# A vision block on one core: one array for each group's rows, and the issue lists of four engines written anew

## The reference, cut to what matters

```python
h = tok(x, W)                                  # patches @ W.T, class token in front
def attn(x):                                   # on layernorm(h)
    k, v, sr = ln1(x) @ Wk.T, ln1(x) @ Wv.T, sigmoid(ln1(x) @ Wr.T)
    y = bi_wkv(decay / T, first / T, k, v)     # two scans with a running maximum, both ways
    x = x + sr * y @ Wo.T
    return x + sigmoid(ln2(x) @ Wr_f.T) * (square(relu(ln2(x) @ Wk_f.T)) @ Wv_f.T)
h = h + attn(layernorm(h))
h = h + moe(layernorm(h))     # sum over experts of c[t, e] * (silu(x Wg + bg) * (x Wu + bu)) Wd, and the shared one
```

## Time and profile before

| | us |
|---|---|
| median of 3 runs | 268.33 |
| lowest, highest | 268.15, 270.0 |
| the profiled execution, its own time | 268.65 |
| its span, first to last instruction | 266.8 |

### The profile page before, as it was taken

One profiled execution on the slowest core, in us unless ns is written; L12 is line 12 of the kernel. 1 busy time (PEld: TensorE's weight loads), 2 busy tenths in 40 slices (PEclk: granted clock), 3 DMA queues, 4 the chain that ended last, 5 costly groups with the idle time before them and its releaser, 6 DMA issues.

```text
span 266.8 us, 4316 instructions
## 1 busy us (share of the span) xinstructions
PE 233.7 (88%) x1436; PEld 211.5 (79%) x1436; DVE 195.0 (73%) x496; ACT 147.6 (55%) x305; POOL 18.0 (7%) x24
## 2 busy tenths in 40 slices
PE   0484968588878999999999999999999999999994
PEld 0373428465557899998999999999999999899993
DVE  4459898999997999989986599877731445654442
ACT  2489886989449997462756894144444332122220
POOL 4100402030011000030010000101000010000000
PEclk9998699999999999999999999999999999999999
DMA  5679550000000280000002430000014510014311
GB/s 150 210 254 337 176 184 2 0 0 0 0 2 1 47 195 2 2 0 0 4 26 68 174 105 4 0 1 0 2 30 160 164 37 2 1 35 106 68 34 37
DMA packets 12823, 17.49 MB, mean 66 GB/s; under 512 B 2144, under 2 KB 10882, under 8 KB 12674
## 3 DMA queue, kind: packets, MB, share of 16 engines
q1 hardware_dynamic: 11272, 16.20, 20.7%
q10 hardware_dynamic: 1530, 1.02, 1.4%
HBM read 16.22 MB, written 0.99 MB: 65 GB/s over the span
## 4 chain that ended last, share of the span: by engine, by line
PE 65%; DVE 16%; ACT 9%; issue 5%; DMA 2%; POOL 1%; SPq 0%; DVEq 0%; POOLq 0%; ACTq 0%
PE PG L958 17%; PE PA L978 15%; PE PG L960 11%; PE PF L978 4%; PE PA L1162 3%; DVE S L721 3%; PE PQ L958 2%; PE PX L995 2%; PE PF L995 2%; DVE K L745 2%; DMA w_tok<-in_w_tok 2%; PE PF L985 1%; DVE S L726 1%; DVE hid L901 1%; POOL rstd L374 1%
## 5 line engine op out<-in xcount | busy, mean ns | idle before, releaser
L553 ACT ACTIVATE act<-PG,columns 128x222 f32<-128x222 f32 (+3 forms) x56 | 28.4, 506 | 63.7 <-PE PG L960 60.0
L958 PE MATMUL PG<-stack,hi_egu 128*128 128x222 f32 (+1 forms) x288 | 62.1, 324 | 0.8 <-DVE hid L901 0.5
L901 DVE SCALAR_TENSOR_TENSOR hid<-PG,columns,act 128x222 f32<-128x222 f32 (+1 forms) x52 | 27.1, 520 | 30.9 <-PE PG L960 15.7
L958 PEld LDWEIGHTS PG<-stack,hi_egu 128*128 128x128 f32 x288 | 45.2, 190 | 4.9 <-DVE hid L901 2.9
L978 PE MATMUL PA<-w_ed,hid 128*124 128x192 f32 (+1 forms) x240 | 46.0, 327 | 0.7 <-DVE hid L914 0.7
L960 PE MATMUL PG<-stack,lo_egu 128*128 128x222 f32 (+1 forms) x192 | 42.7, 304 | 0.0
L978 PEld LDWEIGHTS PA<-w_ed,hid 128*124 128x124 f32 (+1 forms) x240 | 38.6, 183 | 1.1 <-issue 1.0
L960 PEld LDWEIGHTS PG<-stack,lo_egu 128*128 128x128 f32 x192 | 31.7, 190 | 0.0
L374 POOL TENSOR_TENSOR rstd<-var,minus_half 112x2 f32<-112x2 f32 (+3 forms) x12 | 15.2, 1266 | 198.7 <-DVE var L647 198.7
L914 DVE TENSOR_TENSOR hid<-hid,gates 128x222 f32<-128x222 f32 (+1 forms) x48 | 21.7, 463 | 8.2 <-DMA gates<-c_rows 7.4
L978 PE MATMUL PF<-w_down,mix_hid 128*124 128x192 f32 (+1 forms) x120 | 23.2, 327 | 0.2 <-ACT mix_hid L525 0.2
(11 more groups left out here) (230 smaller groups left out, 418.6 us busy)
## 6 DMA issues: line engine op xcount, KB each, us to landing
gates<-in_w_egu SPq DMA_DIRECT2D x6, 512.0 KB, 4.0
gates<-c_rows SPq DMA_DIRECT2D x16, 138.8 KB, 2.8
gates<-c_rows SPq DMA_DIRECT2D x16, 92.5 KB, 2.7
w_ed<-in_w_ed SPq DMA_DIRECT2D x1, 1152.0 KB, 8.0
gates<-c_rows SPq DMA_DIRECT2D x12, 83.2 KB, 2.8
...
```

What stands on the lines that cost most here:

```text
L553: nc.scalar.activation(act[128 - gate:128, n % 2, 0:G.n], PG[0:gate, gate_bank(n), 0:G.n], ACT.Silu, bias=bias).then_inc(act_silu, 1)
L901: V_.scalar_tensor_tensor(out, PG[part, 1, 0:G.n], bias, act[part, i, 0:G.n], ALU.add, ALU.mult).then_inc(mul_done, 1)
L958: mm(out, w_hi[:, slot, cols], x[:, p, 0:G.n], start=(p == 0), stop=False, skip_group_check=True)
```

## The change

1. **One array per group.** `stream[g]` takes the place of `h0`, `base` and `h1`. `x1` adds into it, `h1` adds into it, the experts add into it, and it is stored from there. The two waits named above are gone.
2. **In place.** `norm2` is `x1`, `norm3` is `gate_r`. `Zm` is the front of `V`. ReLU goes from PSUM to `mix_hid` and the square works there in place, so `relu` is gone, and the wait for the mix matmul two before stands ahead of ReLU, not ahead of the square. New waits: `x0` of group g waits for the transposes (not the norm) of M of the group before, and `vt` for the `o` matmuls of the group before.
3. **Gates.** The array holds `HELD` = 4 periods of three chunks, which is all 12 chunks, so slots, DMAs and waits come out as they were. The formulas for tiles and banks also give the same numbers for 2 and 3 tiles.
4. **Queue of SP.** `patches(3)` stands ahead of `gates_across(0)`.
5. **Lists.** The three lists are written anew.

```diff
+        stream = [sb(f"h_{g}", [G.tp, G.tiles, C]) for g, G in enumerate(GROUP)]
-        norm = [None, *(sb(f"norm{i}", [TP, TILES, C]) for i in (1, 2, 3))]
+        norm = [None, sb("norm1", [TP, TILES, C]), x1, gate_r]
-        Zm = sb("Zm", [128, N])
+        Zm = V[:, 0:N]
...
             patches(2)
+            patches(3)
             gates_across(0)
-            patches(3)
...
                 act_e.wait_ge(pe_tok, at(pe_tok, g, bank + 1))
-                if g >= 2 and bank == 0:
-                    act_e.wait_ge(x1_ready, at(x1_ready, g - 2, 1))
...
             yield "kt"
+            since(act_e, pe_o, g)
             tails(V, upper, upper)
...
-            since(act_e, norm_ready[2], g)
+            since(act_e, pe_transposed[2], g)
...
-                nc.scalar.activation(relu[:, 0:G.n], PQ[:, 0:G.n], ACT.Relu).then_inc(act_relu, 1)
-                act_e.wait_ge(act_relu, at(act_relu, g, m + 1))
                 if m >= 2:
                     act_e.wait_ge(pe_mix, at(pe_mix, g, m - 1))
...
+                nc.scalar.activation(mix_hid[:, m % 2, 0:G.n], PQ[:, 0:G.n], ACT.Relu).then_inc(act_relu, 1)
+                act_e.wait_ge(act_relu, at(act_relu, g, m + 1))
+                nc.scalar.activation(mix_hid[:, m % 2, 0:G.n], mix_hid[:, m % 2, 0:G.n], ACT.Square).then_inc(act_square, 1)
...
-            if g >= 2:
-                v.wait_ge(out_stored[g - 2], 16 * GROUP[g - 2].tiles)
...
 ACT_ORDER = _order(
...
-    "F2:exps F2:weights Y0:e6 F3:tok0 Y0:e7 M1:rf M1:mix0 Y0:e8 M1:mix1 Y0:e9 M1:mix2 M1:mix3 M1:mix4 Y0:e10 F3:ln1 M1:mix5",
...
+    "Y0:e5 F3:tok0 M1:rf M1:mix0 Y0:e6 M1:mix1 Y0:e7 F2:weights M1:mix2 Y0:e8 M1:mix3 Y0:e9 M1:mix4 Y0:e10 Y0:e11 F3:ln1",
```

More of the change, by code:

```diff
@@ L41, in __init__ @@
         last = self.n - self.tp
-        self.ts = [0, last] if self.tiles == 2 else [0, last // 4 * 2, last]
-        self.banks = ((0, 0, 2), (1, 2, 3))[:self.tiles - 1]
+        self.ts = [last * t // (2 * (self.tiles - 1)) * 2 for t in range(self.tiles)]
+        self.banks = [(a // 2, a, min(a + 2, self.tiles)) for a in range(0, self.tiles, 2)]
         self.rounds = len(self.banks)
@@ L116, in build, with gate_slot @@
         whole = {name: sb(f"w_{name}", [p, n, C]) for name, p, n in WHOLE}
-        gates = sb("gates", [128, ECH, N])
-        flat_gates = gates[:, :, :].rearrange("p c n -> p (c n)")
-        raw = [flat_gates[:, i * RING_COLS:(i + 1) * RING_COLS] for i in range(RING)]
+        gates_raw = sb("gates", [128, max(3 * HELD * N, RING * RING_COLS)])
+        gates = gates_raw[:, 0:3 * HELD * N].rearrange("p (c n) -> p c n", n=N)
+        raw = [gates_raw[:, i * RING_COLS:(i + 1) * RING_COLS] for i in range(RING)]
+        def gate_slot(g, chunk):
+            return (g * ECH + chunk) % (3 * HELD)
         columns = sb("columns", [128, sum(n for _, n in COLUMNS)])
@@ L140, in build @@
         pat = sb("pat", [128, 2, N])
-        h0 = [sb(f"h0_{i}", [TP, TILES, C]) for i in range(2)]
+        stream = [sb(f"h_{g}", [G.tp, G.tiles, C]) for g, G in enumerate(GROUP)]
         x1, gate_r = (sb(n, [TP, TILES, C]) for n in ("x1", "gate_r"))
-        base, h1 = ([sb(f"{n}_{i}", [TP, TILES, C]) for i in range(2)] for n in ("base", "h1"))
-        norm = [None, *(sb(f"norm{i}", [TP, TILES, C]) for i in (1, 2, 3))]
+        norm = [None, sb("norm1", [TP, TILES, C]), x1, gate_r]
         full = [None, *(sb(f"full{i}", [128, 2, N]) for i in (1, 2))]
@@ L322, in gates_across @@
                     sp.wait_ge(pe_low, len(LOW_ON_PE))
-                    for first, periods, done in ((0, 1, gates_in[0]), (1, PERIODS - 1, gates_in[1])):
+                    for first, periods, done in ((0, 1, gates_in[0]), (1, HELD - 1, gates_in[1])):
                         for chunk, a, b, e in SPANS:
@@ L422, in act_front @@
                 act_e.wait_ge(pe_tok, at(pe_tok, g, bank + 1))
-                if g >= 2 and bank == 0:
-                    act_e.wait_ge(x1_ready, at(x1_ready, g - 2, 1))
-                nc.scalar.activation(h0[g % 2][0:G.tp, a:b, :], rows_of(P[bank], G, a, b), ACT.Copy).then_inc(tok_out, 3 - G.rounds)
+                nc.scalar.activation(stream[g][0:G.tp, a:b, :], rows_of(P[bank], G, a, b), ACT.Copy).then_inc(tok_out, 3 - G.rounds)
                 yield f"tok{bank}"
@@ L485, in act_first_rows @@
             G = GROUP[g]
-            since(act_e, norm_ready[2], g)
+            since(act_e, pe_transposed[2], g)
             act_e.wait_ge(rstd_ready[1], at(rstd_ready[1], g, 1))
             for t in range(G.tiles):
-                last = nc.scalar.activation(x1[0:G.tp, t, :], h0[g % 2][0:G.tp, t, :], ACT.Identity,
+                last = nc.scalar.activation(x1[0:G.tp, t, :], stream[g][0:G.tp, t, :], ACT.Identity,
                                             bias=small[1]["shift"][0:G.tp, 0, t:t + 1], scale=small[1]["rstd"][0:G.tp, 0, t:t + 1])
@@ L673, in dve_front @@
             step, settle, do, settle_apart = steps
-            yield from moments(v, steps, g, 1, h0[g % 2])
+            yield from moments(v, steps, g, 1, stream[g])
             yield "var1"
@@ L794, in dve_mid @@
             settle()
-            step(V_.scalar_tensor_tensor(h[rs], gate_r[rs], 0.5, base[g % 2][rs], ALU.mult, ALU.add))
+            step(V_.scalar_tensor_tensor(x[rs], gate_r[rs], 0.5, x[rs], ALU.mult, ALU.add))
             yield "h1"
             settle()
-            yield from moments(v, steps, g, 3, h)
+            yield from moments(v, steps, g, 3, x)
             yield "var3"
@@ L908, in dve_weighed @@
                 period = (n - SCH) // 3
-                if g == 0:
+                if g == 0 and period < HELD:
                     v.wait_ge(gates_in[min(period, 1)], 16 * len(SPANS))
                 else:
-                    v.wait_ge(gates_in[period], 16 * len(SPANS) * (g + (period < 2)))
+                    v.wait_ge(gates_in[period], 16 * len(SPANS) * (g + (period < 2 or period >= HELD)))
                 out = hid[:, n % 2, 0:G.n]
-                V_.tensor_tensor(out, out, gates[:, n - SCH, 0:G.n], ALU.mult).then_inc(hid_ready, 1)
+                V_.tensor_tensor(out, out, gates[:, gate_slot(g, n - SCH), 0:G.n], ALU.mult).then_inc(hid_ready, 1)
                 yield f"x{n}"
@@ L918, in dve_weighed @@
             for bank, a, b in G.banks:
-                h = h1[g % 2][0:G.tp, a:b, :]
-                last = V_.tensor_tensor(h, h, rows(PA, G, bank, a, b), ALU.add)
+                x = stream[g][0:G.tp, a:b, :]
+                last = V_.tensor_tensor(x, x, rows(PA, G, bank, a, b), ALU.add)
             last.then_inc(out_ready, 1)
@@ L977, in down @@
             for t in range(G.tiles):
-                last = mm(tile_out(P, G, t), src[:, G.ts[t]:G.ts[t] + G.tp], w, start=start and t != 1, stop=stop, skip_group_check=True)
+                last = mm(tile_out(P, G, t), src[:, G.ts[t]:G.ts[t] + G.tp], w, start=start and t % 2 == 0, stop=stop, skip_group_check=True)
             return last
```

25 lines of the change are left out of this document (13 added, 12 removed), and 100 rows, old and new, of tables (ACT_ORDER, DVE_ORDER, PE_ORDER).

## The result

In the first timing the changed kernel took 267.74 us (265.86 to 269.86, 20 runs) against 268.50 (267.84 to 270.70, 20 runs) for the kernel before; the ratio is 0.9942, 95% interval 0.9918 to 0.9967. A second timing gave 267.34 (12 runs) against 269.30 (23 runs), ratio 0.9939 (0.9907 to 0.9970). The ratio leaves out the executions that fell in the chip's slower state, and it is not the quotient of the two medians, which would be 0.9972 and 0.9927. So the kernel is faster by some 0.6%, about 1.6 us (the medians alone differ by 0.8 and by 2.0 us): less than the 1% that I called the limit of a measurement, yet both intervals leave out 1. The prediction was 267.9.

The account below looks back on a forecast made before the run. Group 0's arrival at its experts (80 us, set by DVE), then PE's remaining matmuls were taken as the bound. Terms 0 - 0.4 + 0 + 0.3 = -0.1, taken as -0.4, gave 267.9 us; range 265.5 to 270.9.

Parts of the forecast that it names:

- Bound of the gain: Whole kernel: behind 80 us at most PE's 3.06 us of visible gaps can return; ahead, only what shortens DVE's line.
- my walk: Stepping through the new lists with the old trace's durations, stage by stage; its sum was -0.1 us.
- The arrays: Shared and in-place arrays: dropped and new waits cost 0, `x0` of group 1 bounded at some 0.5 us.
- The front: 0 to 80 us: -0.25 on DVE and +0.25 on ACT, sum 0; `sgu` issued about 18.2, with 1.0 us of cover.
- the -0.25 that I gave to `var1`: Front, DVE: `var1` of group 1 ahead of `sub0` shortens the line that waited 1.22 us for POOL; estimate -0.25 us.
- the first sign that I gave for being right: At the end of the front: PE starts the experts of group 0 within 1 us of 80.
- Start of the experts: 80 to 93 us, walked on to about 103: value 1's 1.05 us wait stays, `cT` idles 0.45; taken -0.4 us.
- Table loads: 94 to 112 us and near 155: four more loads, 5.1 us on ACT, covered by 0.95 and 0.85 us; taken 0.
- loads uncovered: Rival: silus behind the added table loads come late, losing some 4.4 us, 272.3 (at most 273.0); chance 0.15.
- My 10.7 us for loads and drains: ACT's added load by the Trainium skill's account, with a drain of about 1.38 us at each switch; not adopted.
- Behind 112 us: From 112 us to the end: +0.3 us before group 1's third transposes (bounds 0 and +1), group 2 and the end 0.
- the 0.3 us that no row stood for: Whole sum: -0.1 us taken as -0.4, since a list filling one seen gap probably fills others.

Follow-up runs that it names:

- e_norm2: Changed kernel with the three engine lists of before and norm 2 in its own array again; 270.32 us, ratio 1.0014 to the kernel before.
- e_group0: Changed kernel with the lists of before, except the new rows for group 0's expert stage; 267.85 us, ratio 0.9956 to the kernel before.
- e_again: The changed kernel as it is, timed once more; 267.34 us, ratio 0.9939 to the kernel before.
- e_front: Changed kernel with the lists of before, except the new rows up to group 0's first expert gate; 273.19 us, ratio 1.0167 to the kernel before.
- e_loads: Changed kernel with weights of groups 2 and 3 directly behind their exps on ACT, six table loads for ten; 274.92 us, ratio 1.0227 to before.

## Why the prediction came out right, and where it was wrong

**Bound of the gain: wrong.** I wrote that behind 80 us a new list can give back at most the 3.06 us of visible gaps, and my walk gave -0.1, which I made -0.4 on a guess. Behind the first gate 2.5 us came back. Counted from the first gate to the end of the last matmul, PE's visible gaps went only from 2.99 to 2.27 us, its busy time from 180.46 to 178.69. So 1.8 of the 2.5 us lay inside time that the page counts as busy; the amount stayed below my bound, the reason given for the bound was wrong. Rows of PE of before, where I had walked five matmuls of 222 columns with 0.64 us, as from 90.62 to 91.26:

```profile
92.77 0.59 PE L958 MATMUL PG<-stack,hi_egu 128*128 128x222 f32 x3
...
93.64 0.56 PE L958 MATMUL PG<-stack,hi_egu 128*128 128x222 f32 x3
...
121.49 0.59 PE L958 MATMUL PG<-stack,hi_egu 128*128 128x222 f32 x3 [0.32 <-DVE hid L901]
```

From 92.77 to 93.64 is 0.87 us: 0.23 lost, and no bracket says so. Apart from those with a named wait behind them, such groups of stage 0 take 0.55 to 0.69 us from start to next start, except five of before with 0.82 to 0.95 (from 83.13, 85.01, 87.19, 92.77 and 100.05); after has none of that length. Two theories were open, that these short waits or the hand-overs carry the gain; the stages of e_norm2 (52.58, old lists) and e_group0 (51.10) show that group 0's list alone makes 1.5 us of it. Which exchange of rows makes it, and which the 1.1 us in stage 2, was not tried and stays open.

**The arrays: the number 0 wrong with the lists of before, right with the new.** I looked at `x0` of group 1 and gave it a bound of 0.5 us. The step that mattered was `x0` of group 2, with 2.1 us in stage 0, or 3.5 where the clock followed; the new list has `M1:tr2` ahead of it and `F2:rt` between, and no wait stands there (`tr2` at 89.80, `x0` at 92.94 in after). I had priced arrays and lists as if they added up. They don't: the list pays for the array.

**The front: 0 forecast, +1.2 in the profiled execution.** Not by what I weighed. `sgu` was issued at 17.56 (I said 18.2) and nothing waited for it; POOL's 1.22 us stood unchanged, so the -0.25 that I gave to `var1` did not come. The first scan waited 1.49 us for ACT instead of 0.73, in e_again and in after, behind matmuls that ran at half the speed of before's (0.98 for 0.59 us; clock 0.50 from 14 to 24 us). e_norm2 and e_front show that the lists of the front differ by 0.1 us where the matmuls are equally slow. So 0 holds for the lists at a like speed, and my walk took the speed of one execution for a property of the kernel. Whether the new front is slow more often is open, and the medians leave room for it: they fell by 0.8 to 2.0 us, not by the 2.5 won behind the gate. The gates at 81.08 and 82.25 (e_again) also miss the first sign that I gave for being right, a start within 1 us of 80.

**Start of the experts: right in its waits.** The wait before value 1 is 1.03 us (forecast: stays, 1.05). The wait for `cT` is 0.43 (forecast 0.45). Patches at 96.67 without a wait, as said; what it would cost otherwise I had not priced, and it is 7.7 us.

**Table loads: right that they cost 0, with less cover than I walked.** Ten loads of 1283 ns, and the start-to-start step is 1.30 us as in the earlier trace rows:

```profile
98.96 1.28 ACT L556 ACT_TABLE_LOAD   x1
100.26 0.45 ACT L556 ACTIVATE act<-PG,columns 128x222 f32<-128x222 f32 x1
...
110.58 1.28 ACT L556 ACT_TABLE_LOAD   x1
111.88 0.45 ACT L556 ACTIVATE act<-PG,columns 128x222 f32<-128x222 f32 x1
```
```profile
101.22 0.50 PE L959 MATMUL PG<-stack,hi_egu 128*128 128x222 f32 x3
...
112.58 0.62 PE L959 MATMUL PG<-stack,hi_egu 128*128 128x222 f32 x3
```

Silu 5 ended at 100.71 and gate 6 began at 101.22: cover 0.51 for 0.95 walked. Silu 8 ended at 112.33, gate 9 began at 112.58: 0.25 for 0.85. The rival "loads uncovered" was nearer than its price let it seem, and its remedy, fewer loads, would have been wrong: e_loads takes 2.3% more than before. By the Trainium skill, "ScalarE: Activation LUTs", section "What ACT_TABLE_LOAD costs", each switch also drains ACT for about 1.38 us. These rows again show the load and no drain (the silu starts 1.30 us behind the load's start), and with one the cover of 0.25 could not have held. My 10.7 us for loads and drains should read 10.6.

**Behind 112 us: one term can't be read, two stages were wrong.** I counted +0.3 for the third transposes of group 1; it lies within stage 0's -1.6 and can't be read alone. For the gates of group 2 DVE waited 5.84 us where it waited 7.25, and PE not at all, as forecast. Stage 1 lost 0.29, stage 2 won 1.13: I had 0 for both.

The sum came out near (267.9 for 267.74 and 267.34) because a gain taken too small (-0.4 for -2.5) met a loss ahead of the first gate that I had taken as 0: +1.2 in the profiled execution, and 0.5 to 1.7 by the two differences of medians. The two errors had opposite signs, and that was luck. Part of the forecast's closeness is also the 0.3 us that no row stood for.
